# A state-space and expert layer on one core: the place of the gather and the scatter in GpSimd's step, and VectorE's last eight steps written out

## The reference

```python
xn = _layernorm(x, axis=-1)
...
def step(state, inp):                       # 2048 steps, state is [1024 channels, 16]
    dt_t, x_t, B_t, C_t = inp
    dA = jnp.exp(dt_t[..., None] * A)
    dBx = dt_t[..., None] * B_t[:, None, :] * x_t[..., None]
    state = state * dA + dBx
    y = jnp.einsum('bds,bs->bd', state, C_t)
    return (state, y)
...
y = y * jax.nn.silu(gate)
return jnp.einsum('bld,ed->ble', y, out_proj_w)
...
buf = jnp.zeros((E, CAP + 1, H), x.dtype).at[flat_i, slot].set(x[token_ids])
g = jnp.einsum('ech,ehi->eci', buf, w_gate)
u = jnp.einsum('ech,ehi->eci', buf, w_up)
y = jnp.einsum('eci,eih->ech', jax.nn.silu(g) * u, w_down)
```

## Time and profile before

| | |
|---|---|
| median of 3 runs | 1342.65 us (1342.62 to 1343.42) |
| the profiled execution | 1335.79 us |
| its span in the trace | 1334.0 us |
| granted TensorE clock, mean | 0.988 |
| busy: PE | 1254.7 us (94%) |
| busy: DVE | 1079.7 us (81%) |
| busy: ACT | 899.2 us (67%) |
| busy: POOL | 866.5 us (65%) |

### The profile page before, as it was taken

How to read it: one execution, slowest core, us unless ns; L and a number is a source line. 1 busy time by engine, 2 the same in 40 slices (tenths; PEclk the granted TensorE clock), 3 DMA queues, 4 the chain that set the end, 5 groups by cost and what they waited for, 6 DMA issues and landing times.

```text
span 1334.0 us, 52998 instructions
## 1 busy us (share of the span) xinstructions
PE 1254.7 (94%) x21558; PEld 804.3 (60%) x21558; DVE 1079.7 (81%) x1235; ACT 899.2 (67%) x1925; POOL 866.5 (65%) x456
## 2 busy tenths in 40 slices
PE   6899999699999899999899999899999999999998
PEld 4777767455555455555455555455545678787876
DVE  5879889699899889998899999799999474646554
ACT  4666676487888878888788888678787242424343
POOL 3445458289889889898888988889989240303030
PEclk9999999799999999999999999999999999999999
DMA  8363554789999989999999999978898844032130
GB/s 271 124 258 129 213 213 141 242 264 281 308 265 318 287 228 318 293 274 306 267 286 301 268 307 289 311 253 270 260 315 264 281 161 154 36 106 84 64 125 31
DMA packets 131362, 305.64 MB, mean 229 GB/s; under 512 B 18272, under 2 KB 22368, under 8 KB 129504
## 3 DMA queue, kind: packets, MB, share of 16 engines
q1 hardware_dynamic: 123664, 285.92, 65.6%
q0 software_dynamic: 7632, 18.91, 7.1%
HBM read 213.78 MB, written 57.43 MB: 203 GB/s over the span
## 4 chain that ended last, share of the span: by engine, by line
PE 57%; DVE 9%; issue 7%; ACT 5%; DMA 2%; POOL 1%; ACTq 1%; DVEq 0%; SPq 0%; POOLq 0%
PE p_dBx L1367 16%; PE p_dBx L1425 7%; PE p_y L1376 7%; PE p_g L1353 6%; DVE state L1056 5%; PE p_g L1336 5%; PE p_u L1336 3%; PE p_y L1436 3%; PE p_g L1436 2%; PE p_u L1436 2%; PE p_dt L1436 2%; ACT dA L1206 2%; DVE out_operand_parts L1091 2%; DMA dt_blocks_even<-step_rows 1%; PE p_u L1322 1%
## 5 line engine op out<-in xcount | busy, mean ns | idle before, releaser
L1056 DVE TENSOR_TENSOR_SCAN state<-dA,state_carry,p_dBx 128x512 f32<-128x512 f32 x512 | 618.5, 1262 | 61.8 <-PE p_dBx L1367 61.5
L992 POOL TENSOR_TENSOR h_times_C<-state,C_bcast 128x1024 f32<-128x1024 f32 x128 | 304.3, 2379 | 63.1 <-DVE state L1056 62.1
L992 POOL TENSOR_TENSOR C_bcast<-state,C_bcast 128x1024 f32<-128x1024 f32 x128 | 315.9, 2624 | 23.1 <-DVE state L1056 22.4
L1367 PE MATMUL p_dBx<-B_diagonals,step_rows 64*32 64x128 f32 x16384 | 302.6, 275 | 24.4 <-DVE state L1056 12.9
L1367 PEld LDWEIGHTS p_dBx<-B_diagonals,step_rows 64*32 64x32 f32 x16384 | 235.3, 106 | 145.9 <-issue 142.7
L1206 ACT ACTIVATE dA<-dt_blocks_even,A_par 128x512 f32<-128x512 f32 x256 | 169.5, 709 | 27.5 <-DMA dt_blocks_even<-step_rows 27.5
L1206 ACT ACTIVATE dA<-dt_blocks_odd,A_par 128x512 f32<-128x512 f32 x256 | 169.5, 710 | 18.4 <-DMA dt_blocks_odd<-step_rows 16.2
L320 POOL TENSOR_TENSOR w_in_parts_lo<-C_bcast,w_in_parts_hi 128x512 fp32r<-128x512 f32 x64 | 94.4, 1477 | 99.2 <-ACT w_in_parts_hi L538 98.9
L1006 POOL TENSOR_TENSOR step_rows<-step_rows 128x512 f32<-128x512 f32 x16 | 22.5, 1435 | 182.4 <-DMA step_rows<-moe 182.4
L417 DVE SCALAR_TENSOR_TENSOR conv_out<-conv_in,conv_w,conv_out 128x512 f32<-128x512 f32 x96 | 107.2, 1124 | 20.7 <-ACT conv_out L562 18.4
L1353 PE MATMUL p_g<-w_down_pair,step_rows 128*64 128x512 f32 (+1 forms) x396 | 92.5, 602 | 0.0
(11 more groups left out here) (185 smaller groups left out, 2020.9 us busy)
## 6 DMA issues: line engine op xcount, KB each, us to landing
w_gate_pair<-in_w_gate SPq DMA_DIRECT2D x32, 1408.0 KB
w_up_pair<-in_w_up SPq DMA_DIRECT2D x32, 1408.0 KB
w_down_pair<-in_w_down SPq DMA_DIRECT2D x66, 512.0 KB
dt_blocks_odd<-step_rows SPq DMA_DIRECT2D x256, 64.0 KB
dt_blocks_even<-step_rows SPq DMA_DIRECT2D x240, 64.0 KB
w_down_pair<-in_w_down SPq DMA_DIRECT2D x33, 384.0 KB
g_d<-y_gated SPq DMA_DIRECT2D x33, 256.0 KB
sz_d<-silu_gate SPq DMA_DIRECT2D x32, 256.0 KB, 2.2
```

The source lines that it names most:

```text
L992: pool.tensor_tensor(hc[m][:, b, :, :], hb[:, q, :, :], Cb[:, NM * (c % 2) + GS * m:NM * (c % 2) + GS * m + GS, :], ALU.mult).then_inc(s_h ...
L1056: ins = dve.tensor_tensor_scan(hb[:, g % NBUF, s, :], dA[:, g % NBUF, s, :], pB[:, g % 2, :].rearrange("p (t s) -> p s t", s=GS)[:, s, :], ...
L1367: ins = pe.matmul(out[DB * p:DB * p + DB, half, j, :, :], dtxT[k, j * P + DB * b:j * P + DB * b + DB], diag[k, ND * cp + 2 * j + p // 2, a ...
```

## The change

Three edits, all in stage 2:

1. GpSimd waits for `s_xT` and issues the gather for the next step in front of the step's first h*C product. Before, both stood behind it. They also stand in front of the wait for `s_C`.
2. The scatter goes from behind the product of group 4 to behind the product of group 5.
3. VectorE's loop body becomes a function `steps(c, j)`. The first three chunks call it within the loop as before; for the last chunk, four calls with a plain number j write the eight steps out, so that all their addresses are fixed.

```diff
-GATHER_AT, SCATTER_AT = 0, 4
+SCATTER_AT = 5
...
             for i in range(STEPS):
                 c = i // ND
+                pool.wait_ge(s_xT, i + 1)
+                gather(i + 1)
                 pool.wait_ge(s_C, 32 * ND * (c + 1))
                 for g in range(NG):
...
-                    if g == GATHER_AT:
-                        pool.wait_ge(s_xT, i + 1)
-                        gather(i + 1)
                     if g == SCATTER_AT:
                         scatter(i)
...
-            for c in range(NCH):
+            def steps(c, j):
+
+                for u in range(2):
+                    i = ND * c + (2 * j + u)
...
-                                dve.tensor_tensor(xp[1][:, bass.ds(j, 1), :], xT[:, bass.ds(j, 1), :], xp[0][:, bass.ds(j, 1), :],
-                                                  ALU.subtract).then_inc(s_xlo, 1)
+                            dve.tensor_tensor(xp[1][:, j, :], xT[:, j, :], xp[0][:, j, :], ALU.subtract).then_inc(s_xlo, 1)
...
+            for c in range(NCH - 1):
                 with dve.Fori(0, ND // 2) as j:
...
+                    steps(c, j)
+            for j in range(ND // 2):
+                steps(NCH - 1, j)
```

More of the change, by code:

```diff
@@ new lines, in steps @@
+            def steps(c, j):
+                for u in range(2):
+                    i = ND * c + (2 * j + u)
+                    for g in range(NG):
+                        dve.wait_ge(s_hc, NG * i + (g + 1))
+                        dve.wait_ge(s_cry, NG * i + (g + 1))
+                        dve.wait_ge(s_dA, NG * i + (g + 1))
+                        dve.wait_ge(s_bps, NG * i + (g + 2))
+                        for s in range(GS):
+                            n = GS * g + s
+                            ins = dve.tensor_tensor_scan(
+                                hb[:, g % NBUF, s, :], dA[:, g % NBUF, s, :],
+                                pB[:, g % 2, :].rearrange("p (t s) -> p s t", s=GS)[:, s, :],
+                                carry[:, bass.ds(i, 1), n:n + 1].rearrange("p a b -> p (a b)"), ALU.mult, ALU.add)
+                        ins.then_inc(s_scan, 1)
+                        if g == DT_AT:
+                            next_dt(i + 1)
+                            next_dtx(i + 1, 1 - u)
+                        if g == GATE_AT:
+                            gate(i, 1 - u)
+                        if g == X_LO_AT and c == NCH - 1 and u == 1:
+                            dve.wait_ge(s_xhi, j + 1)
+                            dve.tensor_tensor(xp[1][:, j, :], xT[:, j, :], xp[0][:, j, :], ALU.subtract).then_inc(s_xlo, 1)
+                        if g == HH_AT:
+                            dve.wait_ge(s_sg, i + 1)
+                            dve.wait_ge(s_hTps, i + 1)
+                            dve.tensor_tensor(hh[:, :], sg[:, :], pG[:, 0:I], ALU.mult).then_inc(s_hg, 1)
+                        if g == HH_AT + 1:
+                            dve.wait_ge(s_ups, i + 2)
+                            dve.wait_ge(s_hg, i + 1)
+                            dve.tensor_tensor(hh[:, :], hh[:, :], pU[:, 0:I], ALU.mult).then_inc(s_hh, 1)
```

29 lines of the change are left out of this document (removed).

## The result

| | before | after |
|---|---|---|
| median, 4 runs each | 1342.63 us (1336.81 to 1343.42) | 1362.68 us (1360.53 to 1363.92) |
| ratio, 95% interval | | 1.0143 (1.0107 to 1.0180) |
| the profiled execution | 1335.79 us | 1362.60 us |
| its span | 1334.0 us | 1360.8 us |
| granted clock, mean | 0.988 | 0.972 |

The forecast was 1325 us, a gain of 17. The change costs 20 us.

A forecast was written before the change was run, and what follows sets the result against it. The recurrence's steps were taken to be lengthened by holes in TensorE's stream behind GpSimd's gather. -20.2 + 5.5 - 1.5 (VectorE's wait and the scatter) - 1.0 = -17.2 us, from 1342.65 to 1325 us; own range 1319 to 1333, overall 1312 to 1340.

The forecast's parts named there:

- What bounds it: Recurrence, 780 of 1334 us: four parties with almost no slack; most steps take 23.2 to 24.2 us, clean ones 22.7.
- the holes: TensorE's stream runs dry behind the gather's start, lengthening p_y by 15.5 us and dBx 2 by 4.7, together 20.2.
- Part 1: Gather at the step's front, about 0.6 us into the gate product, where its hole is harmless: -20.2 us, bounds 0 and 20.2.
- rival C: Holes move to worse places, dBx 2 and the next dBx 0, if the gather starts late: 1363 us, chance 0.09.
- part 2: Scatter one group later, at about 20.5 us of the step, within `down`: its hole is harmless there, no loss counted.
- What is late next: dt_x waits for `xt_for_dtx`, which a shorter step needs 1.1 us sooner: +5.5 us, bounds 0 and +13.
- Part 3: VectorE's written-out steps in the last chunk save register instructions before scans: -1 us; fetching the longer program 0, bound +4.
- rival A: The transfers bound the step: dt_x 0.6 us late in all 22 steps, step settles at 23.3, 1336 us, chance 0.18.
- PE and ACT never wait on anyone: Skill's rule, read as: a transfer issued by GpSimd could not slow TensorE, so the gain would be nothing.

The follow-up runs named there:

- gather_second: The kernel before with the gather behind the second h*C product instead of the first: 1340.1 us in its one run; repeated on one more chip, 0.9982.
- gather_front: The kernel before with only the gather moved in front of the step's first h*C product: 1333.7 us, 0.9935; repeated on another chip, 0.9967.
- scatter_later: The kernel before with only the scatter moved from behind the product of group 4 to behind that of group 5: 1362.67 us, 1.0157.
- after_xt_first: The changed kernel with SyncE issuing `xt_for_dtx` ahead of the up weights instead of behind them: 1337.96 us, 0.9976 of the kernel before.
- before_again: The kernel before, unchanged, timed against itself: 0.9979.
- gather_front_scatter3: The kernel before with the gather in front of the first product and the scatter one group earlier, behind the product of group 3: 1.0036.
- before_xt_first: The kernel before with only `xt_for_dtx` issued ahead of the up weights: 0.9955; repeated on another chip in more rounds, 0.9979.

## Why the prediction was wrong

**What bounds it, and the holes: right.** p_y over C_bcast takes 62.2 us and not 78.1, gather_second moved the hole into dBx 3, and gather_front alone is faster. Also as forecast, dBx 7 is no longer lengthened (at full clock in no step by over 0.1 us, in 20 before), `down` keeps its 2.80 us at full clock beside the scatter, and VectorE's pause between g = 1 and g = 2 is 1.3 us in place of 2.0 in the steps where dt_x is on time.

**Part 1's place: half right.** Forecast was a gather 0.6 us into the gate product with part 1 alone, and 0.9 to 1.3 with the later scatter. In gather_front the median is 0.6, and dBx 2 is clean in all steps. In the changed kernel it is 1.7, and 1.85 at 388.72 (386.87). It is more than the 1.7 us that rival C named in 16 of the 32 steps, and in exactly these dBx 2 is longer, by 0.13 to 0.57 us (1.38 us in all at 389.38), where the other 16 have 1.16. The sum is 5.9 us, where 4.7 were. So rival C's place was right for half of the steps, at a small price.

**The step that failed: part 2, "The next place is at about 20.5 us of the step, which is within `down` ... harmless in the same way", priced at 0.** It was priced by what TensorE issues at that moment. The scatter is also a transfer of 0.26 MB. In a short step its new place is 1.1 us ahead of the issue of `xt_for_dtx` (382.23 and 383.33), in a long one about 2 us behind it, and in both it runs beside this transfer. scatter_later measures the term alone: +21 us. With the transfer swapped in front of the up weights the late scatter costs nothing that can be measured (1.0002, and 0.9979 for the same kernel with the scatter at its old place). The traffic shows it. Here are the DMA queues while a scatter is in flight: in the kernel before, 5.1 us from 591.5, and below it in the kernel after, 9.0 us from 382.2 (packets, MB, share of the 16 engines):

```profile
q0 software_dynamic: 144, 0.26, 40.9%
q1 hardware_dynamic: 369, 0.58, 40.4%
```

```profile
q1 hardware_dynamic: 712, 2.20, 74.5%
q0 software_dynamic: 144, 0.26, 17.1%
```

Before, it filled a lull: SyncE was busy issuing the 16 small transfers of `spread_dt`, the engines moved 0.58 MB beside it. One group later it runs beside the up weights, `xt_for_dtx` and the down weights, 2.20 MB, and both the scatter (8.8 us for 5.0) and `xt_for_dtx` (9.6 for 7.6) land later.

**What is late next: the right transfer, the wrong size.** The prediction named `xt_for_dtx` and took +5.5 us, bounds 0 to +13. Its wait grew from 11.4 to 44.2 us, because the bound was drawn from a landing time that was held fixed at that of before. The prediction looked at the demand (a step 1.1 us shorter) and not at the supply (a landing 2 us later). And it did not see that the clock falls while TensorE stands still, which made the 3.9 us of waiting at 342.97 a step longer by 6.0. (Over stage 2 the mean granted clock is 0.97 here, 0.99 before, and 0.98 in after_xt_first, whose time is that of before; so not all of the slow stretches cost time.)

With the gather alone at the front the term is mis-sized too. 20.2 us of holes went and 4 to 9 us were gained, so what is late next costs 11 to 16 us, not 5.5, if the holes passed through one for one as forecast. The rows have the places: +7 and +9 at dt_x, +12 and +31 at dA in the two pairs of traces. dA waits for `dt_blocks` and had no term in the sum. What each of these waits costs is not shown, since three traces of one kernel, the one before, already differ by 12 us at dA (34.0 to 45.9; before_again has 37.7). That is the outcome of rival A (the transfers bound the step, 1336 us; measured 1333.7 and 1338.1), with dA beside dt_x as the place.

**Part 3: right within what can be measured** (-1 us; 1.0010, 0.9979 to 1.0041).

**The sum by what was measured:** part 1 -4 to -9, part 2 +21, part 3 about 0, so +12 to +17, against +20. What is left is as large as the error of the terms.

**The rivals.** C had 1363 us and the sign, but its mechanism is not what made the loss: the scatter's hole did not lengthen the next dBx 0 (1.16 us in all steps), the gather's in dBx 2 costs 1 us more than before, and in after_xt_first, where it is 2 us, nothing is lost. Its number was right by chance.

**"PE and ACT never wait on anyone".** The Trainium skill (SBUF — State Buffer, section "Who interferes with whom") says so, of the ports of SBUF. If it is read as the prediction read it, that a transfer issued by GpSimd can't slow TensorE, the runs don't agree: the hole stands in p_y (before, 16.9 to 24.2 us), in dBx 3 (gather_second, 16 us) or in dBx 6 (gather_front_scatter3, 16 us), each time behind the indirect transfer. Whether a port has to do with it no run shows.

**What stays open.** Why before_xt_first has no hole in p_y in one trace and 19.5 us of it in another. It is not the 0.2 us of shift that decided in the earlier trace rows, since p_y is clean with the gather 0.23 us ahead of it; whether the chip or the execution does it was not settled. What makes the hole at all is not shown either, only that it follows the transfer. How much of the second trace's smaller dA wait comes from that was not tried. And why part 1 and the swap gain so little although the holes and dt_x's wait are gone was narrowed to dA's wait for `dt_blocks` (53.6 to 80.0 us against 34.0 to 45.9), but no run took that wait away.

## What to carry to other kernels

An indirect transfer that is moved has two places: one in its engine's stream, one among the transfers in flight. Before you price the second at nothing, list what the other queues issue in the 10 us behind its new place, and which of these has a consumer without slack. Here a swap of two issues on SyncE decided over 21 us, while the edit itself was worth 9 at most.

Where the prediction names the transfer that will be late next, ask whether the change also makes it land later, and not only whether it is wanted sooner.

Of the kernels tried, gather_front is the best against its own reference (0.9935 and 0.9967 on two chips). before_xt_first (0.9955 and 0.9979) can't be told from it, nor its second value from the unchanged kernel (0.9979). The two together (0.9994, against 0.9955 for the swap on that chip) were no better.

## What was unexpected of the hardware

Two transfers in flight together slowed each other more than their size says. A 256 KB scatter that adds took 5.0 us in the lull and 8.8 us beside the weights, and it put 2.2 us on a 256 KB load issued within some 2 us of it (7.6 to 9.8). At the 321 GB/s that the engines moved in the 9.8 us of such a load, 0.26 MB are 0.8 us (an estimate). Written without adding the scatter takes 7.4 us and puts 1.2 us on the load. In the lull its packets took 40.9% of the engines' time for 0.26 MB, about what 0.58 MB of the other queue took.

The order of two issues 0.5 us apart on one queue was worth 3.1 to 4.8 us of landing: behind 1.4 MB of up weights `xt_for_dtx` lands after 7.5 to 9.8 us, ahead of them after 4.2 to 5.2.

A stall of TensorE can cost more than itself. Around 3.47 us of idleness the granted clock was 0.50 for some 6.8 us, and the up product took 3.94 us in place of 2.59; of the 6.0 us by which that step is longer, 3.9 are the wait.
